# Second attention of a fused transformer block: the weighted add of the expert rows moves from VectorE to GpSimd, and the output bias moves into the scatter

## The reference, cut to what matters

```python
x = x + attn_a(layernorm(x), ...)     # linear attention with a causal mask, 16 heads
x = x + ffn(layernorm(x), ...)        # 16 experts, 2 per token, limited capacity
x = x + attn_b(layernorm(x), ...)     # sparse attention, below
x = x + ffn(layernorm(x), ...)        # the same experts again
```

```python
Q, K, V = proj(wq, bq), proj(wk, bk), proj(wv, bv)
scores = einsum('bhqd,bhkd->bhqk', Q, K) * scale
u = 6                                               # int(log(512))
top_u = top_k(scores.max(axis=-1), u)[1]            # the 6 queries with the largest score
attn = softmax(einsum('bhud,bhkd->bhuk', Q[top_u], K) * scale)
padded = zeros(...).at[b, h, top_u].set(einsum('bhuk,bhkd->bhud', attn, V))
out = padded @ wo.T + bo                            # bo is added to every token
```

## Time and profile before

| | |
|---|---|
| median of 3 runs | 1403.18 us (1398.74 to 1406.71) |
| the profiled execution | 1396.88 us |
| its span, first to last instruction | 1395.1 us |
| TensorE matmul busy | 1239.1 us, 89% |
| VectorE busy | 1042.0 us, 75% |
| ScalarE busy | 756.4 us, 54% |
| GpSimd busy | 836.4 us, 60% |
| mean granted TensorE clock | 0.936 of 2.4 GHz |

### The profile page before, as it was taken

The page is one execution under the profiler, slowest core; times in us unless marked ns, Lnnn a source line. Parts: engine busy times, 40 slices in busy tenths (PEclk is TensorE's granted clock), DMA queues, the critical chain, the costliest instruction groups (busy, mean ns, idle before and its releaser), DMA issues.

```text
span 1395.1 us, 28372 instructions
## 1 busy us (share of the span) xinstructions
PE 1239.1 (89%) x8534; PEld 787.4 (56%) x8534; DVE 1042.0 (75%) x4462; ACT 756.4 (54%) x1901; POOL 836.4 (60%) x1246
## 2 busy tenths in 40 slices
PE   3999998996999999999999999999999999999100
PEld 1566665565898965454545445545455469888100
DVE  2899999895674458898999989989998856565322
ACT  2444444442665767666676756656676546556000
POOL 3237776777525224356777767766874445367776
PEclk9999999997999998998999989999999899999655
DMA  6845602011556520000100001011000125466522
GB/s 174 259 154 192 197 30 87 28 44 60 171 163 210 166 65 16 14 11 24 32 25 29 32 24 32 29 62 48 29 28 14 44 79 162 150 218 205 150 75 75
DMA packets 119783, 125.80 MB, mean 90 GB/s; under 512 B 15568, under 2 KB 109904, under 8 KB 119632
## 3 DMA queue, kind: packets, MB, share of 16 engines
q1 hardware_dynamic: 103248, 90.42, 20.5%
q0 software_dynamic: 16384, 33.59, 7.9%
HBM read 50.15 MB, written 73.79 MB: 89 GB/s over the span
## 4 chain that ended last, share of the span: by engine, by line
PE 70%; DVE 12%; POOL 7%; issue 4%; DMA 2%; ACT 2%; SPq 0%; POOLq 0%; ACTq 0%; DVEq 0%
PE pair L1897 25%; PE pair L1823 8%; POOL vmyg L564 6%; PE pair L1685 5%; DVE pT L1401 5%; PE bank L1709 4%; PE pair L1834 4%; PE pair L1812 2%; PE bank L1630 2%; PE bank L1624 2%; PE pair L1674 2%; DVE xs L1318 2%; PE bank L1936 1%; PE bank L1916 1%; PE pair L1695 1%
## 5 line engine op out<-in xcount | busy, mean ns | idle before, releaser
L1897 PE MATMUL pair<-kT,apart 32*128 32x512 f32 x2048 | 460.2, 672 | 3.5 <-DVE smax L1401 2.0
L1401 DVE CUSTOM_DVE_ANT_0 pT<-pair,pT 128x256 f32<-128x256 f32 x1024 | 384.2, 416 | 76.1 <-ACT pT L925 70.4
L925 ACT ACTIVATE pT<-pair 128x256 f32<-128x256 f32 x1024 | 327.0, 397 | 196.8 <-PE pair L1897 193.3
L1897 PEld LDWEIGHTS pair<-kT,apart 32*128 32x128 f32 x2048 | 192.8, 192 | 128.1 <-DVE smax L1401 78.7
L564 POOL DMA_INDIRECT vmyg<-ybufA,slg x128 | 123.7, 966 | 110.6 <-DVE smax L1401 67.9
L1823 PE MATMUL pair<-xeT,unit_w 128*128 128x256 f32 x768 | 184.6, 384 | 0.0
L564 POOL DMA_INDIRECT vmyg<-ybufB,slg x128 | 122.8, 959 | 71.3 <-DVE smax L1401 33.6
L509 POOL DMA_INDIRECT dispB<-xnf,sli x128 | 129.3, 1010 | 57.0 <-issue 35.2
L509 POOL DMA_INDIRECT dispA<-xnf,sli x128 | 130.0, 1016 | 50.9 <-issue 30.2
L1128 DVE TENSOR_TENSOR pT<-pair,causal 128x1024 f32<-128x1024 f32 x128 | 151.2, 1213 | 12.1 <-PE pair L1685 11.2
L1293 DVE TENSOR_TENSOR hid<-sg,pair 128x512 f32<-128x512 f32 x96 | 65.7, 685 | 123.3 <-ACT sg L851 123.1
(11 more groups left out here) (231 smaller groups left out, 1947.6 us busy)
## 6 DMA issues: line engine op xcount, KB each, us to landing
dispB<-zeros SPq DMA_DIRECT2D x16, 1408.0 KB
apart<-dispA SPq DMA_DIRECT2D x96, 128.0 KB
ybufA<-ye SPq DMA_DIRECT2D x48, 256.0 KB
apart<-dispB SPq DMA_DIRECT2D x96, 128.0 KB
ybufB<-ye SPq DMA_DIRECT2D x48, 256.0 KB
dispA<-zeros SPq DMA_DIRECT2D x33, 128.0 KB
xs<-in_x SPq DMA_DIRECT2D x16, 256.0 KB, 3.1
out<-xs SPq DMA_DIRECT2D x15, 256.0 KB, 2.6
```

The source lines that it names most:

```text
L925: act.activation(rel[n % RING][:, q, :], pair[n % RING][:, q, HALF:SEQ], ACT.Relu).then_inc(s["relu_done"], 1)
L1401: dve.tensor_tensor_reduce(out=rel[n % RING][:, q, :], in0=pair[n % RING][:, q, 0:HALF], in1=rel[n % RING][:, q, :], scale=1.0, scalar=LOW ...
L1897: pe.matmul(pair[n % RING][:, q, :], apart[h][at, j, t * P:(t + 1) * P], kTs[h][at, HALF:], start=True, stop=True).then_inc(s["bsc_done"], 1)
```

## The change

Three parts.

1. In bodies 0 to 13 VectorE no longer combines the expert rows. GpSimd does, in `add_rows`: one product of all eight gathered tiles with their weights, in place, and two adds of four tiles each into `xs`. It stands behind the sends of tile 0 and ahead of `key_differences`. VectorE's statistics at n = 22 wait for GpSimd's `combined` instead of its own.
2. The output bias is no longer added by GpSimd. Slot 7 of head 0 (`BIAS_SLOT`), a padded one, is made to match every token: the row of `tokrow` on its partition is -1, as its index is. The image of the value bias `voutb` gets the bias in that row, by one more matmul with `b_bo`, which is now zero except in that row; a copy of `block8` with that column cleared, `blockc`, keeps other parts out of the slot. The wait of `residual` for the bias goes.
3. At the start GpSimd has a memset of `b_bo`, a copy into `blockc`, a select over `tokrow` and a small memset more; SyncE loads `b_bo` as one row, behind the loads of x.

```diff
@@ -54,6 +54,7 @@
 CALLS = B + 3
 LNMAX = -(-K * CAP // UR)
 NF = 3
+BIAS_SLOT = SLOTU - 1
 
 
 def build(nc, w, out):
...
@@ -115,6 +116,7 @@
         eiota = sb("eiota", [P, E])
         tokcol = sb("tokcol", [P, TB])
         tokrow = sb("tokrow", [P, SEQ])
+        blockc = sb("blockc", [P, P])
         unitcol = sb("unitcol", [P, 1])
         mstep = sb("mstep", [P, LNMAX])
         ebase = sb("ebase", [P, E])
...
@@ -359,13 +361,13 @@
                              (b_wv[:, :], w["b_wvT"]), (b_wo[:, :], w["b_woT"]),
                              (cols[:, 3:4], w["b_bq"].rearrange("(p a) -> p a", a=1)),
                              (cols[:, 4:5], w["b_bk"].rearrange("(p a) -> p a", a=1)),
-                             (cols[:, 6:7], w["b_bv"].rearrange("(p a) -> p a", a=1)),
-                             (b_bo[:, :], w["b_bo"].rearrange("(a n) -> a n", a=1).to_broadcast([P, D]))):
+                             (cols[:, 6:7], w["b_bv"].rearrange("(p a) -> p a", a=1))):
                 sp.dma_start(dst, src).then_inc(s["w_in2"], 16)
             with sp.Fori(1, B // 2 - 1) as i:
                 for h in range(2):
                     x_ahead(i, h)
-            sp.wait_ge(s["consts1"], 1)
+            sp.wait_ge(s["consts1"], 2)
+            sp.dma_start(b_bo[BIAS_SLOT:BIAS_SLOT + 1, :], w["b_bo"].rearrange("(a n) -> a n", a=1)).then_inc(s["w_in2"], 16)
 
             for area in disp:
                 sp.dma_start(area[DUMMY:DUMMY + UR, :].rearrange("(p a) d -> p (a d)", a=UT), zeros[:, :]).then_inc(s["zeroed"], 16)
...
@@ -455,6 +457,7 @@
             pool.memset(ident[:, :], 0.0)
             pool.memset(ones[:, :], 1.0)
             pool.memset(onesb[:, :], 1.0)
+            pool.memset(b_bo[:, :], 0.0).then_inc(s["consts1"], 1)
             pool.memset(zeros[:, :], 0.0).then_inc(s["consts1"], 1)
             pool.memset(block8[:, :], 1.0)
             pool.memset(causal[:, :], 1.0)
...
@@ -484,14 +487,20 @@
                                pattern=[[-DH, H], [0, DH]], channel_multiplier=1).then_inc(s["ms1"], 1)
             pool.wait_ge(s["ms1"], 1)
             pool.affine_select(out=bv, in_=bv, compare_op=ALU.is_ge, fill=0.0, base=DH - 1,
-                               pattern=[[DH, H], [0, DH]], channel_multiplier=-1)
+                               pattern=[[DH, H], [0, DH]], channel_multiplier=-1).then_inc(s["ms2"], 1)
 
             def iota(t, base, pattern, cm):
                 return pool.iota(t, base=base, pattern=pattern, channel_multiplier=cm,
                                  allow_small_or_imprecise_dtypes=True)
             iota(eiota[:, :], 0, [[1, E]], 0)
             iota(tokcol[:, :], 0, [[P, TB]], 1)
-            iota(tokrow[:, :], 0, [[1, SEQ]], 0)
+            iota(tokrow[:, :], 0, [[1, SEQ]], 0).then_inc(s["ms2"], 1)
+            pool.wait_ge(s["ms2"], 2)
+            pool.tensor_copy(blockc[:, :], block8[:, :]).then_inc(s["ms2"], 1)
+            pool.affine_select(out=tokrow[:, :], in_=tokrow[:, :], compare_op=ALU.not_equal, fill=-1.0, base=-BIAS_SLOT,
+                               pattern=[[0, SEQ]], channel_multiplier=1).then_inc(s["ms2"], 1)
+            pool.wait_ge(s["ms2"], 4)
+            pool.memset(blockc[:, BIAS_SLOT:BIAS_SLOT + 1], 0.0)
             iota(unitcol[:, :], 0, [[1, 1]], 1)
             iota(mstep[:, :], 0, [[UR, LNMAX]], 0)
             iota(ebase[:, :], CAP, [[SPAN, E]], 0).then_inc(s["consts2"], 1)
...
@@ -668,6 +677,20 @@
                 pool.wait_ge(s["bkT_ready"], n + 1)
                 pool.tensor_tensor(kTs[k][:, SEQ:], kTs[k][:, 0:HALF], kTs[k][:, HALF:SEQ], ALU.subtract).then_inc(s["kdiff_done"], 1)
 
+            def add_rows(b, h):
+
+                pool.wait_ge(s[f"got{h}"], (b // 2 + 1) * 16 * TB * K)
+                at = slice(b * TB * K, (b + 1) * TB * K)
+                pool.tensor_tensor(yg[h][:, :, :], yg[h][:, :, :], wts[:, at].unsqueeze(2).to_broadcast([P, TB * K, D]),
+                                   ALU.mult).then_inc(s["weighted"], 1)
+                pool.wait_ge(s["weighted"], b - 1)
+                xb = xs[:, tiles_of(b), :]
+                yk = yg[h][:, :, :].rearrange("p (t k) d -> p t k d", k=K)
+                for k in range(K):
+                    if k:
+                        pool.wait_ge(s["comb0"], b + 1)
+                    pool.tensor_tensor(xb, xb, yk[:, :, k, :], ALU.add).then_inc(s["combined" if k else "comb0"], 1)
+
             def normed(b, n, dst, kind, q, call):
 
                 pool.wait_ge(s["rstd_ready"], call + 1)
...
@@ -699,6 +722,7 @@
                     if b + 2 == HALFB:
                         stored(1)
                     pair_made(1)
+                    pool.wait_ge(s["combined"], b + 1)
                     fetch(b + 2, h, (0, 1))
                 if b >= 3:
                     places(b - 3, b - 3 + B, 1 - h)
...
@@ -715,10 +739,11 @@
                     norm_scale(ffn_call(b - 2), TB)
                     normed(b - 2, b - 2 + B, xnf[(b - 2 + B) % NF], "ffn", 0, ffn_call(b - 2))
                 send_tile(16, 0)
+                if fetch_:
+                    add_rows(b + 2, h)
                 if next:
                     key_differences(b + 1, 1 - h)
                 send_tile(20, 1)
-                add_bias(b, b + B, b_bo)
                 if fetch_:
                     norm_scale(att_call(b + 2), TB)
                     normed(b + 2, b + 2 + B, xnb[(x + 2) % 4], "att", 0, att_call(b + 2))
...
@@ -1372,7 +1397,7 @@
                     indices(1, 1)
                     dve.wait_ge(s["w_in2"], 16 * 11)
                     dve.tensor_scalar(qbias[:, :], inturn[:, :], cols[:, 3:4], None, ALU.mult).then_inc(s["qbias_done"], 1)
-                    dve.tensor_scalar(vbias[:, :], block8[:, :], cols[:, 6:7], None, ALU.mult).then_inc(s["vbias_done"], 1)
+                    dve.tensor_scalar(vbias[:, :], blockc[:, :], cols[:, 6:7], None, ALU.mult).then_inc(s["vbias_done"], 1)
                 if 16 <= g < 19:
                     table_slots(1, (g - 16,))
 
...
@@ -1444,7 +1469,7 @@
                 dve.wait_ge(s["aexp_done"], b + 1)
                 dve.reciprocal(ainv[:, :], asum[:, :]).then_inc(s["ainv_done"], 1)
                 dve.wait_ge(s["cx_done"], b + 1)
-                dve.tensor_tensor(cxm[:, :], bank[1][:, 0:P], block8[:, :], ALU.mult).then_inc(s["cx_ready"], 1)
+                dve.tensor_tensor(cxm[:, :], bank[1][:, 0:P], blockc[:, :], ALU.mult).then_inc(s["cx_ready"], 1)
 
             def context_out(b):
                 dve.wait_ge(s["cw_done"], b + 1)
...
@@ -1453,7 +1478,6 @@
                                          op0=ALU.mult, op1=ALU.add).then_inc(s["cw_ready"], 1)
 
             def residual(b):
-                dve.wait_ge(s["bias_added"], b + B + 1)
                 dve.wait_ge(s["bo_done"], b + 1)
                 xb = xs[:, tiles_of(b), :]
                 dve.tensor_tensor(xb, xb, bank[1][:, :].rearrange("p (t d) -> p t d", t=TB), ALU.add).then_inc(s["x1_ready"], 1)
...
@@ -1495,10 +1519,6 @@
                         selected_q(b - 1)
                     if last and n == 18:
                         selected_max(b - 1)
-                    if fetch and n in (18, 19):
-                        add_first(b + 2, h, ((0, 1), (2, 3))[n - 18])
-                    if fetch and n in (20, 21):
-                        add_second(b + 2, h, ((0, 1), (2, 3))[n - 20])
                     if fetch and n == 22:
                         dve.wait_ge(s["combined"], b + 3)
                         dve.wait_ge(s["moments"], att_call(b + 2))
...
@@ -2021,7 +2041,8 @@
             def start_b(g):
                 if g == 1:
                     pe.wait_ge(s["vbias_done"], 1)
-                    pe.matmul(bank[1][:, 0:D], vbias[:, :], b_wo[:, :], start=True, stop=True).then_inc(s["vout_done"], 1)
+                    pe.matmul(bank[1][:, 0:D], vbias[:, :], b_wo[:, :], start=True, stop=False)
+                    pe.matmul(bank[1][:, 0:D], ident[:, :], b_bo[:, :], start=False, stop=True).then_inc(s["vout_done"], 1)
                 if g == 12:
                     turn(B, "att", xnb[0])
                 if g == 13:
```

More of the change, by code:

```diff
@@ L231, in build @@
         bank = [pb(f"bank{i}") for i in range(2)] + [pair[i // 2][:, i % 2, :] for i in range(2 * RING)]
-        names = ("w_in w_in2 vm_zero consts1 consts2 consts3 headof_done qbias_done ms0 ms1 wnr x_in0 x_in1 bias_added " + " ".join(f"{k}_{n}" for k in ("att", "ffn") for n in "xn_ready tp_done xT_ready".split()) + " stats moments rs rstd_ready "
+        names = ("w_in w_in2 vm_zero consts1 consts2 consts3 headof_done qbias_done ms0 ms1 ms2 wnr x_in0 x_in1 bias_added " + " ".join(f"{k}_{n}" for k in ("att", "ffn") for n in "xn_ready tp_done xT_ready".split()) + " stats moments rs rstd_ready "
                  ""
@@ L238, in build @@
                  "xe_in0 xe_in1 xe_tp xeT_ready unit_w_ready gu_done silu_done hid_done y_done y_ready xe_in2 xe_in3 y_out0 y_out1 "
```

(2 more changed lines are left out.)

## The result

The changed kernel takes 1407.54 us, the median of 20 runs (1401.49 to 1419.21), against 1401.69 us for the kernel before in 20 runs (1397.10 to 1407.76): a ratio of 1.0049 with a 95% interval of 1.0026 to 1.0071, about 6 us slower. A second set of 12 runs gave 1.0045. The forecast was 1408, reckoned from the 1403.18 of three runs before; the 20 runs put the kernel before 1.5 us lower. Every ratio here is of fast runs alone, so two of the 12 runs of e1_early, at 1414 and 1415 us, are in its median but not in its ratio.

The account below looks back on a forecast made before the run. Each second-attention batch was read as a TensorE part hiding the adds, then a VectorE part. Lateness 6.6 + matmul 0.4 - body 0's 2.2 = +4.8 us on the median 1403.2 gave 1408; range 1395 to 1423.

Parts of the forecast that it names:

- What is removed: Second attention, bodies 3 to 13: VectorE's adds, 3.0 us per batch, lie beside TensorE's work, so no gain was taken.
- 0.26: Second attention: TensorE's visible wait for VectorE beside the adds, 0.26 us per batch, kept only for the range.
- rival E: Handover in time, TensorE's 0.26 us per batch comes back, two clock falls stay away: 1391 us, chance 0.16.
- The price of the product and the adds: Added GpSimd work per batch: product 1.89 us, two adds 2.58, waits between 0.16, together 4.63 us.
- Handover and lateness: Statistics behind pair 22: VectorE waits for GpSimd, reaches pair 26 0.63 us late; 0.6 for each of 11 bodies, 6.6 us.
- one for one: From pair 26 on, any lateness of VectorE lengthens the batch by the same amount.
- rival B: GpSimd hands over much later, as with a send's 1.42 us gap; lateness 1.7 to 2.2 us: 1423 us, chance 0.15.
- Body 0: First body of the second attention: VectorE's adds are links of the chain there, so removing them gains 2.2 us.
- The rest: One matmul more at 431 us costs about 0.4 us; GpSimd's constants at the start and the bias load cost nothing.
- Rival C: VectorE's stall takes work from TensorE, three more batches run partly at 1.2 GHz: 1419 us, chance 0.14.

Follow-up runs that it names:

- e1_early: The changed kernel with add_rows moved ahead of the sends of tile 0: 1400.37 us, ratio 0.9969 to the kernel before.
- e5_thin: The kernel before with VectorE's eight multiply-adds in bodies 0 to 13 cut to one column each: 1399.92 us, ratio 0.9983.
- e7_after_again: The changed kernel measured again without any edit, 12 runs: 1407.20 us, ratio 1.0045 to the kernel before.
- e3: The kernel before with only the adds moved from VectorE to GpSimd, its bias add kept: 1404.07 us, ratio 1.0012.
- e4: The changed kernel with the adds given back to VectorE, so only the bias part and constants differ from before: 1403.81 us, ratio 0.9996.
- e6_mid: The changed kernel with add_rows moved behind the key difference: 1436.06 us, ratio 1.0245 to the kernel before.
- e2_late: The changed kernel with add_rows moved behind the key difference and the sends of tile 1: 1481.84 us, ratio 1.0558 to the kernel before.
- e8_early_bias_kept: The kernel before with the adds on GpSimd ahead of the sends of tile 0, its bias add kept: 1403.93 us, ratio 1.0020.

## Why the prediction was right, and where it was not

The sign, the place and the size of the total were right: GpSimd hands over late, VectorE stands still for 2.9 us ahead of the statistics (forecast: about 3), and the kernel gets 6 us slower (forecast: 4.8). That the total came so close is in part luck: the term for an ordinary batch was three times too large, and bodies with a gap and a lower clock, which the sum left out, made up for it. By the steps:

- **What is removed is hidden in bodies 3 to 13**: shown, by e5_thin (38.29) and by e1_early (38.30). There was no 0.26 to be won either, and rival E's road to 1391 was closed.
- **The price of the product and the adds**: 1.91 and 2 x 1.27 us against 1.89 and 2 x 1.29. The 2.25 that the prediction had estimated from the Trainium skill (GPSIMD Engine Reference, section 3.1) does not hold for an operand that repeats one value over 128 elements.
- **Handover and lateness**: the term "0.63 us late, 0.6 for each of the 11 bodies, 6.6 us" was mis-sized. At pair 26 it was 0.28, and the batch is 0.18 longer (38.46 us, where the forecast had 38.9). Three parts were too dear. The second send took 0.98 us instead of 1.11, so the product began 0.13 earlier (714.70 + 5.33 = 720.03 against the assumed 720.16), and the rest of the handover came 0.04 sooner. From the statistics to pair 26 VectorE needed 3.50 us (722.82 - 719.32), not 3.68, since pair 25's maxima follow without a break. And of the 0.28 some 0.1 was taken back in TensorE's next eight matmuls (2.29 us against 2.39), which the step "one for one" denied.
- **The other lateness, rival B**: its gap ahead of the second send came in bodies 6 and 12, the same two as before, and not as a rule. Body 6 costs 39.63 - 38.28 = 1.35 us in e7_after_again; body 12, always beside a slow stretch, I put at the same. Bodies 3, 4, 11 and 13 showed 0.2, 0.5, 0.9 and 0.3. With 0.18 for each of the other five that is 0.9 + 1.9 + 2.7 = 5.5 us over the 11 bodies. The forecast had 6.6, evenly spread.
- **Body 0**: "2.2 us" was too much; e3 against e4 gives about 0.9 at full clock. Together 5.5 - 0.9 = +4.6, where the forecast had +4.4.
- **The rest** (a matmul, constants, the load of the bias): nothing that can be measured, by e4_bias_only.
- **Rival C, the clock**, stood beside the sum and belonged in it. Within the 12 or more timed runs of a kernel here a run's time falls by 8 to 11 us when its mean granted clock is 0.01 higher. The mean over the runs was 0.929 for before (57 runs), 0.925 for after (32 runs), 0.909 for e6_mid and 0.895 for e2_late. For after that would be 3 to 4 of the 6 us.

The last two accounts don't close. The bodies sum to 4.6 us, the clock takes 3 to 4, and 6 were measured, so some 2 us are counted twice or lie within the error of either. Body 11's 0.9 is in both: its clock was 0.97 and 0.98 in the two profiles, against 1.00 in before. Nor does the stall alone say how often the clock falls: e3_adds_only has after's wait and dearer batches (38.6), but a mean clock of 0.930, and only 1.7 us more than before. And e4_bias_only, which has no such stall, had six of the bodies 3 to 13 at a mean clock of 0.92 or less in its one profile, where after had four, e7_after_again and e3_adds_only three each and before two. What decides, for stalls of 3 us, in which batches TensorE drops to 1.2 GHz stays open. With e6_mid's stall of 3.6 us and e2_late's of 6.1 the clock fell in nearly every batch; that the stall brings it about is argued from these two kernels and, for e2_late, the order of its rows; no run changed the clock alone.

## What to carry to other kernels

Where work is hidden on one engine, as it was in bodies 3 to 13, taking it away gained nothing here, and giving it to another engine could lose; what counted was when its result is handed over, and one step earlier in the receiving queue was worth 7 us by the medians (e1_early against after). Size a lateness at the point where the waiting engine had idle time of its own, not at the wait: 2.9 us of waiting cost 0.18, and the next 0.72 us cost 0.75. Where TensorE is near its full rate, put a price on the clock as well: of the time that the longer stalls of e6_mid and e2_late cost, about half or more went with stretches at half rate.

## What the runs showed of the hardware that was not expected

- In e2_late a pause in TensorE's work, once in each batch and mostly 2.4 to 2.7 us long, was followed by slower matmuls: behind the longest, of 3.50 us, four took 2.42 us instead of 1.13, with a granted clock of 0.64 over that stretch. In e6_mid TensorE was idle for at most 0.6 us in each of the bodies 3 to 13 but body 6 (1.2 us), and yet ten of eleven batches had a slow stretch: about 12 us by the batches at full clock, 34 measured.
- The two indirect DMAs of GpSimd that send tile 0 are 0.30 us apart, but 1.42 or 1.43 in bodies 6 and 12 of before and of after. The same two bodies show a gap in all ten profiles; in e1_early and e8_early_bias_kept, where the adds stand ahead of these sends, it is 1.19 or 1.20. Its cause was not found.
- A product with one input that repeats a value over 128 elements costs GpSimd 1.91 us for 1024 elements per partition; an add of two full inputs costs 1.27 for 512.
- A cast of 128x8 on VectorE took 466 ns in e8_early_bias_kept and 271 in e1_early beside GpSimd's norm, and 142 in before without it.
